# One pass for the distances' product, fp32 operands for the adjacency's product, in a two-layer graph network on one core

## What is computed

```python
# layer 0
h   = relu(layernorm(x))
adj_hat = adj + eye(n);  d = deg ** -0.5
agg = einsum('bnm,bmf->bnf', d[:, :, None] * adj_hat * d[:, None, :], h)
x   = x + relu(agg @ W.T + b)
# layer 1, on h = relu(layernorm(x))
s    = h @ w_se.T + b_se                       # 3 columns a node
sq   = sum(s * s, axis=-1)
dist = sq[:, :, None] + sq[:, None, :] - 2 * einsum('bnd,bmd->bnm', s, s)
A    = exp(-dist) * adj
x_nmp = A @ relu(h @ w_msg.T + b_msg)
# beside it a 17-tap convolution over the nodes (done here by a discrete Fourier transform),
# then a GRU-like gate of [x_conv, x_nmp] and h
```

## Time and profile before

| | us |
|---|---|
| median of 3 runs | 1836.18 (1833.64 to 1838.35) |
| the profiled execution | 1836.6 |
| its span | 1834.8 |
| PE busy | 1793.7 (98%) |
| DVE busy | 1194.6 (65%) |
| ACT busy | 1033.0 (56%) |
| POOL busy | 879.0 (48%) |

### The profile page before, as it was taken

The page is one execution under the profiler, slowest core; times in us unless marked ns, Lnnn a source line. Parts: engine busy times, 40 slices in busy tenths (PEclk is TensorE's granted clock), DMA queues, the critical chain, the costliest instruction groups (busy, mean ns, idle before and its releaser), DMA issues.

```text
span 1834.8 us, 30613 instructions
## 1 busy us (share of the span) xinstructions
PE 1793.7 (98%) x10580; PEld 1598.0 (87%) x10580; DVE 1194.6 (65%) x2238; ACT 1033.0 (56%) x1844; POOL 879.0 (48%) x1053
## 2 busy tenths in 40 slices
PE   5999999999999999999989999999999999999998
PEld 5999999999999989999878888888888888888886
DVE  8899999999888845556775445445445545545544
ACT  5989899889898976665533323323323323323332
POOL 6788888888777736656632212212212212212211
PEclk9999999999999999999999999999999999999999
DMA  6465566566555436766864353454454454444342
GB/s 202 138 208 192 196 204 202 198 199 210 195 194 182 150 146 147 178 162 164 213 176 101 101 121 80 102 120 83 102 118 85 101 117 89 99 116 88 99 108 41
DMA packets 513816, 262.61 MB, mean 143 GB/s; under 512 B 365575, under 2 KB 473479, under 8 KB 513662
## 3 DMA queue, kind: packets, MB, share of 16 engines
q1 hardware_dynamic: 512606, 260.52, 51.7%
q10 hardware_dynamic: 1056, 0.13, 0.0%
HBM read 151.51 MB, written 109.05 MB: 142 GB/s over the span
## 4 chain that ended last, share of the span: by engine, by line
PE 95%; DVE 2%; issue 1%; ACT 1%; DMA 0%; POOL 0%; SPq 0%; ACTq 0%; DVEq 0%; POOLq 0%
PE P L113 75%; PE P L912 5%; PE P L618 4%; PE P L666 4%; PE P L779 3%; PE P L645 3%; PE P L637 2%; DVE wgl L869 0%; DVE yo L804 0%; DVE wh0l L754 0%; DMA col<-in_cols 0%; DMA yt<-y_d 0%; DVE wh2l L754 0%; DVE wsum L742 0%; ACT hd L394 0%
## 5 line engine op out<-in xcount | busy, mean ns | idle before, releaser
L894 POOL TENSOR_TENSOR xnx1l<-xnf,xnx1h 128x1024 fp32r<-128x1024 f32 x16 | 44.0, 2749 | 348.2 <-ACT xnx1h L887 348.2
L894 POOL TENSOR_TENSOR xnx0l<-xnf,xnx0h 128x1024 fp32r<-128x1024 f32 x15 | 41.6, 2772 | 317.8 <-ACT xnx0h L887 317.8
L993 ACT ACTIVATE tr<-P,cold 128x512 f32<-128x512 f32 x64 | 44.2, 691 | 193.9 <-PE P L113 193.9
L996 ACT ACTIVATE nn<-gn,col 128x512 f32<-128x512 f32 x64 | 46.4, 725 | 179.2 <-DVE gn L1010 179.2
L1017 DVE SCALAR_TENSOR_TENSOR tz<-tz,tr 128x512 f32<-128x512 f32 x64 | 44.3, 692 | 148.0 <-ACT tz L1000 147.9
L548 POOL TENSOR_TENSOR axl<-af,axh 128x512 fp32r<-128x512 f32 x64 | 93.0, 1453 | 99.2 <-ACT axh L374 99.2
L1000 ACT ACTIVATE tz<-P,cold 128x512 f32<-128x512 f32 x64 | 44.1, 689 | 162.2 <-PE P L113 162.2
L1006 DVE SCALAR_TENSOR_TENSOR gn<-tr,gn 128x512 f32<-128x512 f32 x64 | 44.7, 699 | 127.2 <-ACT tr L993 127.2
L113 PE MATMUL P<-w1mh,xxh 128*128 128x512 f32 x256 | 108.0, 422 | 0.0
L912 PEld LDWEIGHTS P<-gt,yt 128*128 128x128 f32 x768 | 98.8, 189 | 5.9 <-DMA yt<-y_d 1.1
L912 PE MATMUL P<-gt,yt 128*128 128x136 f32 (+1 forms) x768 | 101.2, 281 | 0.4 <-DMA yt<-y_d 0.3
(11 more groups left out here) (202 smaller groups left out, 6840.0 us busy)
## 6 DMA issues: line engine op xcount, KB each, us to landing
xh_d<-xst SPq DMA_DIRECT2D x64, 320.0 KB, 5.1
xl<-xh_d SPq DMA_DIRECT2D x40, 512.0 KB, 6.2
y_d<-yo SPq DMA_DIRECT2D x80, 256.0 KB, 2.5
x<-in_x SPq DMA_DIRECT2D x64, 256.0 KB, 3.0
a<-in_adj SPq DMA_DIRECT2D x64, 256.0 KB, 4.4
at<-in_adjt SPq DMA_DIRECT2D x64, 256.0 KB, 4.6
x_d<-x SPq DMA_DIRECT2D x64, 256.0 KB, 4.9
xn_d<-xt SPq DMA_DIRECT2D x64, 256.0 KB, 5.0
```

The costliest lines, as they stand in the source:

```text
L894: e.e.tensor_tensor(o[1][:, :, :], xnf[p % 2][:, :, :, :].rearrange("p c i t -> p c (i t)"), o[0][:, :, :], ALU.subtract).then_inc(done, 1)
```

## The change

The distances' product becomes one pass. ACT now writes `uvf` (fp32) where it wrote `uv`. DVE rounds it to `uvh` (float32r), and then makes the two operands `uv` = uvh x low + uvf in float32r, with a column `low` of 0 or -1 a row: a row with 0 is the value itself, rounded; one with -1 is what the rounding left. The rows of s and of its squares stand three and two times in each group of 32, as high and as low halves, so that one matmul of 96 rows holds high x high, high x low and low x high. The product moves from the end of PE's turn for batch i-5 to the head of the next turn (batch i-6). DVE does its three new instructions behind the norm statistics of x2, and the copy of the spectrum's second half goes from DVE to ACT. The transposes wait for `uvf` instead of `uv`.

The adjacency's product takes `hd` and `ah` as they are, 4 fp32 matmuls for 12; the four splits (ACT L321, L353; DVE L416; POOL L553) go, and `hd` and `ah` get two buffers each.

```diff
--- before.py
+++ after.py
@@ -155,7 +155,7 @@
-        bse = col[:, 28:29]
+        bse, low_u, low_v = col[:, 28:29], col[:, 29:30], col[:, 30:31]
@@ -174,11 +174,8 @@
-        hdx = p1.hl("hdx", [128, 2, 256])
-        ajh = [p1(f"ajh{i}", [128, 512], F32R) for i in range(2)]
-        ajl = [p1(f"ajl{i}", [128, 512], F32R) for i in range(2)]
-        hd = p1("hd", [128, 2, 256])
-        ah = p1("ah", [128, 512])
+        hd = [p1(f"hd{i}", [128, 2, 256]) for i in range(2)]
+        ah = [p1(f"ah{i}", [128, 512]) for i in range(2)]
@@ -209,7 +206,10 @@
-        uv = p1("uv", [128, 2, 256])
+        uvf = p1("uvf", [128, 2, 256])
+        uvh = p1("uvh", [128, 2, 256], F32R)
+        uv = p1("uv", [128, 2, 256], F32R)
@@ first_scalar @@
-            if live(i, 2):
-                b = i - 2
-                e.wait_ge(S["hd"], b + 1)
-                e.wait_ge(S["agg"], b)
-                e.e.copy(hdx[0][:, :, :], hd[:, :, :]).then_inc(S["hdhi"], 1)
...
-            if live(i, 1):
-                b = i - 1
-                e.wait_ge(S["ah"], b + 1)
-                e.wait_ge(S["agg"], b - 1)
-                e.e.copy(ajh[b % 2][:, :], ah[:, :]).then_inc(S["ajhi"], 1)
...
                 e.wait_ge(S["s"], b + 1)
-                e.wait_ge(S["dist"], b)
+                e.wait_ge(S["uv"], b)
...
             if live(i, 7):
-                spectrum_out(e, i - 7, 0)
+                for c in range(2):
+                    spectrum_out(e, i - 7, c)
...
@@ first_vector @@
-            if live(i, 2):
-                b = i - 2
-                e.wait_ge(S["hdhi"], b + 1)
-                e.wait_ge(S["agg"], b)
-                e.e.tensor_tensor(hdx[1][:, :, :], hd[:, :, :], hdx[0][:, :, :], ALU.subtract).then_inc(S["hdlo"], 1)
...
-            if live(i, 7):
-                spectrum_out(e, i - 7, 1)
...
+            if live(i, 5):
+                b = i - 5
+                e.wait_ge(S["uvf"], b + 1)
+                e.wait_ge(S["uv"], b)
+                e.e.tensor_scalar(uvh[0:96, :, :], uvf[0:96, :, :], 1.0, None, ALU.mult).then_inc(S["uvh"], 1)
+                e.wait_ge(S["uvh"], b + 1)
+                e.wait_ge(S["dist"], b)
+                for k, low in ((0, low_u), (1, low_v)):
+                    t = e.e.scalar_tensor_tensor(out=uv[0:96, k, :], in0=uvh[0:96, k, :], scalar=low[0:96, :],
+                                                 in1=uvf[0:96, k, :], op0=ALU.mult, op1=ALU.add)
+                t.then_inc(S["uv"], 1)
@@ first_gpsimd @@
-            if live(i, 1):
-                b = i - 1
-                e.wait_ge(S["ajhi"], b + 1)
-                e.wait_ge(S["agg"], b - 1)
-                e.e.tensor_tensor(ajl[b % 2][:, :], ah[:, :], ajh[b % 2][:, :], ALU.subtract).then_inc(S["ajlo"], 1)
@@ first_tensor @@
+            if live(i, 6):
+                b = i - 6
+                e.wait_ge(S["uv"], b + 1)
+                e.wait_ge(S["af"], b)
+                for m in range(2):
+                    t = e.e.matmul(P[DIST][:, m * 256:m * 256 + 256], uv[0:96, 0, m * 128:m * 128 + 128],
+                                   uv[0:96, 1, :], start=True, stop=True, skip_group_check=True)
+                t.then_inc(S["dist"], 1)
...
-                e.wait_ge(S["hdhi"], b + 1)
-                e.wait_ge(S["hdlo"], b + 1)
-                e.wait_ge(S["ajhi"], b + 1)
-                e.wait_ge(S["ajlo"], b + 1)
+                e.wait_ge(S["hd"], b + 1)
+                e.wait_ge(S["ah"], b + 1)
                 e.wait_ge(S["aglo"], b)
                 for f in range(2):
-                    t = multiply(e.e, mm3([{m: h[:, m, f * 128:f * 128 + 128] for m in range(2)} for h in hdx],
-                                          [{m: h[b % 2][:, m * 256:m * 256 + 256] for m in range(2)}
-                                           for h in (ajh, ajl)],
-                                          P[AG][:, f * 256:f * 256 + 256], True, True, [(0, 0), (1, 1)]))
+                    for m in range(2):
+                        t = e.e.matmul(P[AG][:, f * 256:f * 256 + 256], hd[b % 2][:, m, f * 128:f * 128 + 128],
+                                       ah[b % 2][:, m * 256:m * 256 + 256], start=m == 0, stop=m == 1,
+                                       skip_group_check=True)
                 t.then_inc(S["agg"], 1)
...
-            if live(i, 5):
-                b = i - 5
-                e.wait_ge(S["uv"], b + 1)
-                e.wait_ge(S["af"], b)
-                for m in range(2):
...
@@ block.sync @@
-            sync.dma_start(col[:, 0:29], cols).then_inc(S["col_in"], 16)
+            sync.dma_start(col[:, 0:31], cols).then_inc(S["col_in"], 16)
@@ kernel @@
-    bse = np.zeros((128, 1), np.float32)
-    for base in (0, 32, 64):
-        wse[:, base:base + 3] = a["L1_gnn_w_se"].T
-        bse[base:base + 3, 0] = a["L1_gnn_b_se"]
+    bse = np.zeros((128, 3), np.float32)
+    for base, halves in ((0, ((0, 0), (0, -1), (-1, 0))), (32, ((0, 0), (0, -1))), (64, ((0, 0), (-1, 0)))):
+        for k, half in enumerate(halves):
+            rows_k = slice(base + 3 * k, base + 3 * k + 3)
+            wse[:, rows_k] = a["L1_gnn_w_se"].T
+            bse[rows_k, 0] = a["L1_gnn_b_se"]
+            bse[rows_k, 1:3] = half
```

More of the change, by code:

```diff
@@ L119 @@
 consts crs diag rows normrow w1s chi clo ones taps
-ldx0 ldx1 lda0 lda1 lat0 lat1 st0 ag0a ag0 deg0 degm rs0 dd sd sbias hd hdhi hdlo ah ajhi ajlo agg aghi aglo
-out0 u x2 sx20 sx21 st1 ag1a ag1 rs1 n1b xn xnt xt sxt xxhi xxlo s uv cm0 cm1 tcm0 tcm1 h1 mshi mslo
+ldx0 ldx1 lda0 lda1 lat0 lat1 st0 ag0a ag0 deg0 degm rs0 dd sd sbias hd ah agg aghi aglo
+out0 u x2 sx20 sx21 st1 ag1a ag1 rs1 n1b xn xnt xt sxt xxhi xxlo s uvf uvh uv cm0 cm1 tcm0 tcm1 h1 mshi mslo
 dist af am axhi axlo nmp nm snm dft0 dft1 xe0 xe1 sxh0 sxh1
@@ L310, in spectrum_out @@
             e.wait_ge(S[f"sxh{g % 2}"], 64 * (g // 2))
[L311 to L314, removed]
+            e.e.copy(dst, src).then_inc(S[f"xe{c}"], 1)
         def first_scalar(e, i):
-            if live(i, 2):
-                b = i - 2
-                e.wait_ge(S["hd"], b + 1)
-                e.wait_ge(S["agg"], b)
-                e.e.copy(hdx[0][:, :, :], hd[:, :, :]).then_inc(S["hdhi"], 1)
             if live(i, 5):
@@ L361, in first_scalar @@
                 e.wait_ge(S["s"], b + 1)
-                e.wait_ge(S["dist"], b)
+                e.wait_ge(S["uv"], b)
                 e.wait_ge(S["col_in"], 16)
                 e.wait_ge(S["ones"], 1)
-                e.e.activation(uv[0:32, :, :], P[SXN][0:32, 0:256].unsqueeze(1).broadcast_to((32, 2, 256)),
+                e.e.activation(uvf[0:32, :, :], P[SXN][0:32, 0:256].unsqueeze(1).broadcast_to((32, 2, 256)),
                                ACT.Identity, bias=bse[0:32, :])
-                e.e.activation(uv[32:64, 1, :], P[SXN][32:64, 0:256], ACT.Square, bias=bse[32:64, :])
-                e.e.activation(uv[64:96, 0, :], P[SXN][64:96, 0:256], ACT.Square,
-                               bias=bse[64:96, :]).then_inc(S["uv"], 1)
+                e.e.activation(uvf[32:64, 1, :], P[SXN][32:64, 0:256], ACT.Square, bias=bse[32:64, :])
+                e.e.activation(uvf[64:96, 0, :], P[SXN][64:96, 0:256], ACT.Square,
+                               bias=bse[64:96, :]).then_inc(S["uvf"], 1)
             if live(i, 6):
@@ L391, in first_scalar @@
                 e.wait_ge(S["sbias"], b + 1)
-                e.wait_ge(S["hdlo"], b)
+                e.wait_ge(S["agg"], b - 1)
                 for n in range(2):
-                    t = e.e.activation(hd[:, n, :], xs[b % 5][:, n, :], ACT.Relu,
+                    t = e.e.activation(hd[b % 2][:, n, :], xs[b % 5][:, n, :], ACT.Relu,
                                        bias=m[:, 34 + n:35 + n], scale=m[:, 32 + n:33 + n])
@@ L434, in first_vector @@
                 e.wait_ge(S[f"lat{b % 2}"], loaded(b, 2))
-                e.wait_ge(S["ajlo"], b)
+                e.wait_ge(S["agg"], b - 1)
                 e.wait_ge(S["eye2_in"], 16)
-                e.e.tensor_tensor(ah[:, :], at[b % 7][:, :], eye2[:, :], ALU.add).then_inc(S["ah"], 1)
+                e.e.tensor_tensor(ah[b % 2][:, :], at[b % 7][:, :], eye2[:, :], ALU.add).then_inc(S["ah"], 1)
             if live(i, 3):
@@ L633, in first_tensor @@
                 e.wait_ge(S["xxlo"], b)
-                e.wait_ge(S["uv"], b)
+                e.wait_ge(S["uvf"], b)
                 for c in range(2):
@@ L639, in first_tensor @@
                 t.then_inc(S["xnt"], 1)
-            if live(i, 5):
-                b = i - 5
-                e.wait_ge(S["uv"], b + 1)
-                e.wait_ge(S["af"], b)
-                for m in range(2):
-                    t = e.e.matmul(P[DIST][:, m * 256:m * 256 + 256], uv[0:96, 0, m * 128:m * 128 + 128],
-                                   uv[0:96, 1, :], start=True, stop=True, skip_group_check=True)
-                t.then_inc(S["dist"], 1)
         def unit_parts(n):
@@ L1229, in _ @@
             e.wait_ge(S["s2t"], 2)
```

(4 more changed lines are left out.)

## The result

Four runs of each kernel on one chip: the changed kernel takes **1852.8 us** in the median (1851.56 to 1853.7), the kernel before 1836.01 (1833.64 to 1838.35). The ratio is 1.009, with a 95% interval of 1.0079 to 1.0102: slower by 16.8 us, beyond the 0.3% that counts. The profiled execution of the changed kernel took 1852.58 us (span 1850.8), the one of the kernel before 1836.6 (span 1834.8): 16.0 us in the spans, which the two traces have to explain. The direction was forecast, and the time lies inside the stated range (1833 to 1893), but the forecast was 1872: less than half of the expected 36 us came.

The account below looks back on a forecast made before the run. TensorE bounds the kernel at 10.16 us a turn; its saving is lost to uv's waiting for POOL. Start -1, end -1, turns without taps +3, with taps +35: +36 on 1836.6, less 0.4, gives 1872 us; range 1833 to 1893.

Parts of the forecast that it names:

- The products: On TensorE: adjacency's product 1.72 us for 1.42, distances' product 0.24 for 0.87; turn 9.83 us instead of 10.16.
- The start (-1): First turns, whose chain goes through DVE: hdxl's -2.4 us against dearer adjacency products and DVE's new work; -1 us.
- the end (-1): Last turns, with no adjacency product: both effects nearly cancel, -1 us.
- uvh at 0.45: DVE's new one-input instruction uvh takes 0.45 us, between bounds of 0.41 and 0.69.
- the rival of 0.69: uvh on DVE takes 0.69 us, so ax low is first in all turns: 1888 us; chance 0.15.
- The first and second rival: At uv and ax low: waits don't happen, 1814 us, chance 0.17; uv's too close for POOL, 1836 to 1843, chance 0.15.
- Turns without taps: First uv ahead of POOL's ax low, second behind: turn 10.3 us for 10.16; some 23 turns, +3 us.
- Turns with taps: POOL's multiplication and taps' operation make DVE late; turns alternate 11.9 and 10.3 us, mean 11.1: 37 turns, +35 us.
- The third rival: Taps' turns find a better phase, late turns one in three or less: +12 to +24, 1848 to 1860 us; chance 0.13.
- the rival that ended faster: Both uv's run before ax low, or uv and POOL's operation don't block each other: 1814 us; chance 0.17.
- the blocking for a whole operation: A DVE operation with two SBUF inputs waits out POOL's wide one: 1.58 us for 0.69 in the earlier trace.

Follow-up runs that it names:

- E5: Changed kernel with three POOL moves: multiplication early (after ah), taps' operation ahead of ax low, ax low after both uv's; 1817.71 us, ratio 0.9898.
- E4: Kernel before with only the adjacency's product on fp32 operands and its splits gone; 1849.99 us, ratio 1.0074.
- E1: Changed kernel, but POOL waits for this turn's two uv's before it starts ax low; 1842.27 us, ratio 1.0031.
- E3: Changed kernel with ax low waiting for both uv's and the taps scaled before ax low; 1840.59 us, ratio 1.0023.
- E7: Changed kernel with the adjacency's halves back, so the distances' part alone, hd's low half written over hd; 1949.46 us, ratio 1.0614.
- E10: E7 with the three POOL moves of E5 and the adjacency's low half placed after ms low; 1866.64 us, ratio 1.0164.
- E2: Changed kernel with POOL's taps' operation between its multiplication and ax low instead of behind ax low; 1842.14 us, ratio 1.0027.

## Why the prediction came out as it did

- **The products: right.** 1.73 us for the adjacency (1.72 forecast), 0.24 for the distances (0.24), a turn of 9.84 for PE alone (9.83; E5, and +0.29 for +0.30 in E4).
- **The start (-1) and the end (-1): close.** -1.8 + 0.7 = -1.1 up to the 10th agl. What follows the 64th adds 0.5 where -1 was forecast.
- **uvh at 0.45: right, at the lower bound.** It takes 0.40 to 0.41; the rival of 0.69 is out. The rule of the Trainium skill (VectorE: DVE Perf Modes, What auto-detection actually checks), the mode of two elements a cycle for a single input and an output in SBUF whose outer dimensions are even, had it, and the diagonal's row, which spoke against it, was no guide.
- **The first and second rival: out.** A uv that comes after ax low's start waits for it each time (60 of them, each over 0.28 us after ax low), and there is no steady turn in which both get in first.
- **Turns without taps: mechanism right, 0.1 too dear.** Forecast 10.3, measured 10.20. ax low starts 2.36 us after uvf (forecast +2.35), uvh ends there too, and both uv's follow ax low instead of one ahead and one behind; the next product starts 4.4 after uvf (4.45), uvf 5.8 after the product (5.8). That the other order of ax low and the first uv costs the same was luck.
- **Turns with taps: this is the step that failed**, "the taps' op gets in (5.0), first uv 5.45, second uv 5.9 after a small one: the next turn starts at u + 6.1 = 11.9. After so long a turn POOL is early and DVE free, and the turn is 10.3 again. Mean 11.1". Measured: 10.60, and steady. Three of its terms were off. The taps' operation does get in, but costs the second uv 0.22 us, not 0.9: the pair is 2.03 us in these turns and 1.9 to 2.0 in the others. The hold at L451 adds 0.73, not 1.0. And there is no recovery: POOL's small chain now waits for DVE's aggregates, which stand behind the uv's [the row at 302.33, "<-DVE sm L396"], so that POOL follows DVE at a fixed distance. Its power function meets DVE's ah (1.48 us for 1.01), which makes the multiplication late enough to meet L451, in every turn from 116 us on. I had let POOL run ahead after a long turn, and it can't. With both holds in each turn DVE is simply full, 8.74 + 1.15 + 0.73 = 10.62, and the price is +0.41 a turn instead of +0.94. 37 x 0.53 = 20 us, which is the error of the forecast (1872 for 1852.8); the misses of the smaller terms, +1.5 and -1.5, cancel.
- **The third rival has the number and not the mechanism.** 1852.8 lies in its 1848 to 1860, but it had long turns in one of three or less; measured, all are alike, 0.41 longer each. That its figure fits is luck.
- **A bound that I hadn't written down:** DVE's own sum per turn. I followed the path to the uv's, found the holds, and never added up the engine: 8.74 undisturbed plus the holds is a floor, and in the turns with taps of the changed kernel it was the floor that decided.

E5 also answers to the rival that ended faster (1814 us): it is what the change gives where "the waits don't happen", 1817.7.

## What to carry to other kernels

Where VectorE gets new two-input or tensor_scalar work on the critical path, list POOL's wide operations and what each meets in one turn; a hold cost up to 1.1 us here, most of POOL's 1.3, and POOL's operation moved beside VectorE's PSUM reads, statistics or reductions cost nothing (E5). Removing one hold can only shift it (E1, E3): place all of POOL's wide operations at once, by waits on the VectorE instruction behind which each has to start. And add up each engine's own turn, holds included, beside the path: the turn can't be shorter than the larger of the two. It can be longer: in E3 DVE's sum (8.74 + 0.96 at ms low + 0.13 at L452) and PE's are both 9.83, and the turn is 10.22, with DVE idle for 0.39 us of it, waiting for ACT's high half of xx.

## What of the hardware was not expected

- **A waiting POOL operation gets in between two VectorE operations that stand back to back**, and with operations of 512 columns as well as small ones (E1: x2 runs out, POOL's multiplication goes, ms low takes 1.76 us for 0.68). How long after POOL's end a held VectorE operation ends goes by its own length: 0.02 to 0.03 us for the tiny L451 (0.17 undisturbed), 0.28 for uv and uvh (0.47 and 0.40; the first uv at 510.90 takes 1.56 us and ends 0.28 past ax low), 0.55 for ms low and x2 (0.68; E1, and the earlier trace rows).
- **One input is enough to be held when the operation is a tensor_scalar on SBUF:** uvh takes 0.92 to 0.97 us for 0.40 (E7, E10) and L451, with 2 columns, 0.90 for 0.17, while statistics (0.74 for two, E5) and the reduction (0.67, in the changed kernel at 306.10) keep their length beside POOL's multiplication. The Trainium skill (SBUF — State Buffer, Who interferes with whom) says that tensor_scalar can be held and that tensor_reduce, on this chip, never is; the trace agrees.
- **It goes both ways, and small POOL operations are held too:** the small one behind the power function takes 0.67 us for 0.20 in E5, where it starts beside ms low on VectorE, and the power function 1.48 for 1.01 beside ah.
- **POOL's tensor_scalar holds less than its two-input operations, and not every VectorE operation alike.** The taps' operation (119x256, 0.93 us) holds uvh to its end: in E5 uvh starts 0.60 us after it and is over 0.28 us past it, in each of 37 turns, just as behind aj low in E10. But `ah`, with two inputs in SBUF, starts 0.53 us after it in E1, at nearly the same point, and takes its 0.68 us. What comes early on is held for 0.22 us and no more: x2, 0.11 us after it in E2 (0.91 for 0.68), the tiny L452, 0.12 after it (0.38 for 0.16), and the second uv, 0.22 after it in the changed kernel (0.69 for 0.47). So the blocking for a whole operation, which the prediction took from rows 8, where POOL's operation has two inputs, doesn't hold for this one. Why is open.
